# Softmax attention: the outputs of a head are turned by plain transposes in two halves, and VectorE adds the high and low parts

## The chip, the core and the metric

The kernel runs on one core of one Trainium2 chip. The metric is the device time of one execution in microseconds (us). The engines are TensorE (PE in the profile, its weight loads PEld), VectorE (DVE), ScalarE (ACT), GpSimd (POOL) and SyncE (SP, which issues the DMAs).

## What is computed

Four sublayers run one after the other over 2 x 1024 tokens of width 512: a gated delta-rule attention, a feed-forward with 4-bit weights, a latent attention with rotary embedding and softmax, and a feed-forward with 2:4 sparsity. The change is in the third, in the softmax part:

```python
attn = jnp.einsum('bqhd,bkhd->bhqk', q, k) * scale      # 16 heads, 16 numbers each for q and k
attn = jax.nn.softmax(attn, axis=-1)
out = jnp.einsum('bhqk,bkhd->bqhd', attn, v)            # 32 numbers per head
out = out.reshape(b, s, d)
return out @ wo
```

## The kernel before

`softmax_heads` works through 32 heads (16 heads of 2 sequences), 8 steps to a head, one for each tile of 128 keys or queries (`T` = 8). Each engine has a body written out for four heads (`QUAD`), in which `t` is the step; `passes` runs it once by itself (`first`), six times in a loop, and once more by itself (`last`). The order of the work on each engine is the order in which these bodies are written, and semaphores tie the engines together. In every step

- TensorE computes a tile of raw scores of a later head, 12 tiles ahead (`query_scores`, L1623, into the single PSUM tile `q_scores`). VectorE takes the maximum over the 1024 keys from it (`maximum`, L1557, a reduction of 128x1024). The next `query_scores` waits for that reduction (`max_done`).
- TensorE computes the next tile of transposed scores with the maxima subtracted (`key_scores`, L1639), ScalarE takes the exponential (L1511) and rounds 768 of its 1024 columns to a high part `p_hi` (L1500), and GpSimd computes the remainder `p_lo` (L1459).
- TensorE multiplies a tile of three steps earlier with the values (`output`, L1656 to L1658). The stationary operand holds high values in columns 0 to 31, low values in columns 32 to 63, and ones in 64 and 65. So rows 0 to 31 of the sum are the output by the high values, rows 32 to 63 by the low ones, and row 64 is the denominator.

Once per head the following comes in between. In step 3 of the next head ScalarE and VectorE copy the finished sums, [66 rows x 1024 queries], from PSUM to `out_t` (L1494, L1570). In step 4 TensorE transposes the maxima of the next head (`turn_top`, L1631) into the one PSUM bank `turned`, and VectorE copies them out (`copy_top`, L1564). Ahead of the `query_scores` of step 5, `turn_out` (L1660) waits for that copy and for both copies to `out_t`, and brings the head's sums to query-major form by eight fp32 matmuls (L1667): the stationary operand is a 128x128 block of `out_t`, the moving one is `fold`, [128 x 33], which holds two 32x32 identities above one another and a one for the denominator, so that the matmul turns the block and adds high and low part at once:

```python
for t in range(T):
    last = pe.matmul(turned[:, t * OUT_COLS:(t + 1) * OUT_COLS], out_t[:, t * P:(t + 1) * P], fold[:],
                     start=True, stop=True)
```

In step 6, after that step's reduction, `normalise_head` on VectorE takes the reciprocal of the eight denominators (L1577) and multiplies 128x256 numbers with them into `mixed` (L1580). `fold` is filled in the stage's beginning (L1531, L1545, L1546), and SyncE, TensorE, ScalarE and GpSimd wait for that beginning (`ones_done`).

## Time and profile before

| | us |
|---|---|
| median of 3 runs (3488.66 to 3490.54) | 3490.04 |
| the profiled execution | 3493.09 |
| its span in the trace | 3491.3 |
| attention stage of the change, from its first memset to the last multiplication | about 2177 to 2846.5 |
| of it, TensorE from first to last matmul | 2206.5 to about 2845.8 |

A time in the trace counts from the start of the span. Busy time is given per engine, with its share of the span; the idle time in front of an instruction is given in square brackets with the instruction that ended it. A matmul's recorded duration contains the way through the array, so that successive matmuls overlap in the record and TensorE can look busy where it waited; the start times of its weight loads (PEld) tell its pace.

### The profile page before, as it was taken

The page shows a single profiled execution, that of the slowest core. Times are in us where ns is not written, and L with a number is a line of the kernel's source. Part 1 is how long each engine was busy: PE and PEld are TensorE (multiplying, and loading weights), DVE is VectorE, ACT ScalarE, POOL GpSimd, SP SyncE. Part 2 cuts the span into 40 slices and gives each one's busy share as a digit, 9 for nine tenths or more (in the row PEclk, how much of TensorE's full clock was granted, in tenths as well). Part 3 has the DMA queues.
Part 4 walks back from the last instruction along what each step waited for, and adds up shares of the span by engine and source line. Part 5 has one row for each costly group of instructions (what it writes and reads, how often), then busy time and mean ns, then how long its engine had stood idle before and what let it go on. Part 6 is the DMA issues. An engine that isn't in the chain of part 4 may idle for free. (4 is left out here: it accounts for less than half of the span.)

```text
span 3491.3 us, 44228 instructions
## 1 busy us (share of the span) xinstructions
PE 3107.1 (89%) x16144; PEld 2588.9 (74%) x16144; DVE 1854.5 (53%) x2398; ACT 1176.3 (34%) x1731; POOL 809.2 (23%) x438
## 2 busy tenths in 40 slices
PE   5778888888869999999999965599999986999998
PEld 4667777777758888888888854388888865888887
DVE  5755555555464454454454454466655635554554
ACT  2323333333221121121111112277777752222221
POOL 0023333333200000000000002287888850000000
PEclk8978889999889999999999987699999998999999
DMA  2310000000010010010010002000000001000001
GB/s 93 111 37 20 21 20 21 20 21 7 7 50 23 18 32 22 18 34 20 18 35 19 1 5 114 31 29 27 30 27 28 25 13 48 13 37 24 12 12 48
DMA packets 45623, 104.09 MB, mean 30 GB/s; under 512 B 3600, under 2 KB 24080, under 8 KB 42704
## 3 DMA queue, kind: packets, MB, share of 16 engines
q1 hardware_dynamic: 45520, 102.62, 8.8%
q8 instruction: 76, 1.25, 0.1%
q14 instruction: 27, 0.22, 0.0%
HBM read 80.33 MB, written 22.02 MB: 29 GB/s over the span
## 5 line engine op out<-in xcount | busy, mean ns | idle before, releaser
L1459 POOL TENSOR_TENSOR att_p_lo<-att_probs,att_p_hi 128x768 fp32r<-128x768 f32 x256 | 467.2, 1836 | 159.4 <-ACT att_p_hi L1500 156.3
L1557 DVE TENSOR_REDUCE att_top<-att_q_scores 128x1 f32<-128x1024 f32 x250 | 305.8, 1223 | 240.3 <-PE att_q_scores L1623 233.0
L297 DVE TENSOR_TENSOR fp_hidden<-fp_gelu,fp_up 128x512 f32<-128x512 f32 x128 | 88.0, 687 | 447.9 <-PE fp_up L75 384.0
L1511 ACT ACTIVATE att_probs<-att_k_scores 128x1024 f32<-128x1024 f32 x256 | 262.6, 1026 | 169.4 <-PE att_k_scores L1639 165.2
L116 POOL MEMSET n1a_power<- 128x16 f32 x1 | 0.1, 111 | 1078.0 <-POOLq L52 1078.0
L1623 PE MATMUL att_q_scores<-att_k_stack,att_q_stack 128*128 128x512 f32 x500 | 191.6, 465 | 48.7 <-DMA att_q_stack<-att_k_stack 47.2
L286 DVE TENSOR_TENSOR k_stream<-k_stream,fp_down 128x512 f32<-128x512 f32 x256 | 175.5, 685 | 91.1 <-PE fp_down L75 87.5
L347 ACT ACTIVATE fp_gelu<-fp_gate 128x512 f32<-128x512 f32 x128 | 76.2, 596 | 422.0 <-PE fp_gate L75 421.1
L73 PE MATMUL fp_gate<-f_feat_hi,fp_w_hi 128*128 128x512 f32 x512 | 200.0, 391 | 13.8 <-DVE fp_w_lo L266 13.8
L1500 ACT CAST att_p_hi<-att_probs 128x768 fp32r<-128x768 f32 x256 | 211.5, 827 | 0.0
L808 POOL TENSOR_TENSOR dr_a_l<-dr_a_t,l_mask 128x1536 f32<-128x1536 f32 x48 | 172.1, 3593 | 143.7 <-PE dr_bank L1088 79.1
L74 PE MATMUL fp_gate<-f_feat_lo,fp_w_hi 128*128 128x512 f32 x512 | 199.9, 390 | 0.0
L75 PE MATMUL fp_gate<-f_feat_hi,fp_w_lo 128*128 128x512 f32 x512 | 199.8, 390 | 0.0
L75 PE MATMUL fp_up<-f_feat_hi,fp_w_lo 128*128 128x512 f32 x512 | 199.2, 389 | 0.0
L74 PE MATMUL fp_up<-f_feat_lo,fp_w_hi 128*128 128x512 f32 x512 | 199.2, 389 | 0.0
L73 PE MATMUL fp_down<-fp_w_hi,fp_h_hi 128*128 128x512 f32 x512 | 199.2, 389 | 0.0
L74 PE MATMUL fp_down<-fp_w_lo,fp_h_hi 128*128 128x512 f32 x512 | 199.2, 389 | 0.0
L75 PE MATMUL fp_down<-fp_w_hi,fp_h_lo 128*128 128x512 f32 x512 | 199.2, 389 | 0.0
L73 PE MATMUL fp_up<-f_feat_hi,fp_w_hi 128*128 128x512 f32 x512 | 199.2, 389 | 0.0
L1639 PE MATMUL att_k_scores<-att_q_stack,att_k_stack 128*128 128x512 f32 x512 | 166.7, 407 | 14.5 <-DMA att_q_stack<-att_top_rows 14.0
L957 DVE TENSOR_TENSOR dr_t_m<-dr_t_m,dr_bank 128x512 f32<-128x512 f32 x120 | 82.5, 688 | 180.0 <-PE dr_bank L1097 180.0
L1918 DVE TENSOR_TENSOR sp_hidden<-sp_silu,sp_up 128x512 f32<-128x512 f32 x64 | 43.9, 687 | 222.8 <-PE sp_up L75 221.7
(339 smaller groups left out, 7342.1 us busy)
## 6 DMA issues: line engine op xcount, KB each, us to landing
f_words<-codes SPq DMA_DIRECT2D x16, 768.0 KB
f_scale<-scales SPq DMA_DIRECT2D x16, 768.0 KB
f_staged<-w_sparse SPq DMA_DIRECT2D x12, 1024.0 KB, 4.8
qkv<-pc_rows SPq DMA_DIRECT2D x9, 1024.0 KB, 4.4
dr_raw<-qkv SPq DMA_DIRECT2D x16, 576.0 KB, 6.1
att_q_stack<-rotated SPq DMA_DIRECT2D x64, 128.0 KB
att_k_stack<-rotated SPq DMA_DIRECT2D x64, 128.0 KB
k_stream<-hidden SPq DMA_DIRECT2D x4, 1024.0 KB, 8.9
```

Of the source, the lines that this page charges most:

```text
L73: pe.matmul(out, w_hi, x_hi, start=start, stop=False)
L74: pe.matmul(out, w_hi, x_lo, start=False, stop=False)
L75: return pe.matmul(out, w_lo, x_hi, start=False, stop=stop)
L286: dve.tensor_tensor(tile, tile, down_ps[j][:], ALU.add).then_inc(added, 1)
L297: dve.tensor_tensor(hidden[:, c, :], gelu[:, c, :], up_ps[c][:], ALU.mult).then_inc(product_done, 1)
L808: pool.tensor_tensor(a_l[:, level % 2], a_t[:], const(LEVEL0 + level, BH), ALU.mult).then_inc(a_l_done, 1)
L1459: pool.tensor_tensor(p_lo[:, buffer, :], probs[:, slot, 0:SPLIT], p_hi[:, buffer, :].bitcast(F32), ALU.subtract).then_inc(lo_done, 1)
L1500: act.copy(p_hi[:, buffer, :], probs[:, slot, 0:SPLIT]).then_inc(hi_done, 1)
L1511: act.activation(probs[:, t, :], k_scores[:], ACT.Exp).then_inc(exp_done, 1)
L1557: dve.tensor_reduce(top[buffer][:, STACK + t:STACK + t + 1], scores[:], AX.XY, ALU.max, negate=True).then_inc(max_done, 1)
L1623: last = pe.matmul(scores[:, half, :], q_stack[j][:, t * P:(t + 1) * P], k_stack[j][:, half * TB:(half + 1) * TB], start=True, stop=True)
L1639: last = pe.matmul(k_scores[:, half, :], k_stack[j][:, t * P:(t + 1) * P], q_stack[j][:, half * TB:(half + 1) * TB], start=True, stop=True)
```

## The change

The eight matmuls with `fold` are replaced by eight plain transposes against the identity, each 128x128. Four of them fill the bank `turned` (4 x 128 columns), so that it goes in two halves: half 0 ahead of the `query_scores` of step 5, as before; half 1 ahead of the `query_scores` of step 7, after a wait until VectorE has finished with half 0. Since a transpose doesn't add the parts, VectorE does it. For each half it takes the reciprocal of four denominators, copies the low part from PSUM to SBUF, adds it to the high part within PSUM, and multiplies. Half 0 is done in step 6, half 1 in step 0 of the following head, each after that step's reduction. ScalarE's and VectorE's copies to `out_t` wait for one half each, and `fold` goes away.

```diff
-        fold = s.sb("fold", [P, OUT_COLS])
-        inverse = s.sb("inverse", [P, QTILES])
+        inverse = s.sb("inverse", [P, QTILES // 2])
+        low_part = s.sb("low_part", [P, QTILES // 2, HEAD_DIM1])
...
-            by_query = turned[:, 0:T * OUT_COLS].rearrange("p (t d) -> p t d", d=OUT_COLS)
-
-            def normalise_head(g, n, j):
-                dve.wait_ge(out_turned, g + 1)
-                dve.reciprocal(inverse[:], by_query[:, :, HEAD_DIM1]).then_inc(inverse_done, 1)
-                dve.wait_ge(inverse_done, g + 1)
-                dst = mixed[:, bass.ds(n, 1), :, HEAD_DIM1 * j:HEAD_DIM1 * (j + 1)].rearrange("p o t d -> p (o t) d")
-                dve.tensor_tensor(dst, by_query[:, :, 0:HEAD_DIM1],
-                                  inverse[:].unsqueeze(2).broadcast_to([P, T, HEAD_DIM1]), ALU.mult).then_inc(mixed_done, 1)
+            by_query = turned[:].rearrange("p (t d) -> p t d", t=T // 2)
+            upper, lower = by_query[:, :, 0:HEAD_DIM1], by_query[:, :, HEAD_DIM1:2 * HEAD_DIM1]
+
+            def normalise_half(g, n, j, half):
+                dve.wait_ge(out_turned, 2 * g + half + 1)
+                dve.reciprocal(inverse[:], by_query[:, :, 2 * HEAD_DIM1]).then_inc(inverse_done, 1)
+                dve.tensor_copy(low_part[:], lower).then_inc(lowered, 1)
+                dve.wait_ge(lowered, 2 * g + half + 1)
+                dve.tensor_tensor(upper, upper, low_part[:], ALU.add).then_inc(folded, 1)
+                dve.wait_ge(inverse_done, 2 * g + half + 1)
+                dve.wait_ge(folded, 2 * g + half + 1)
+                tiles = slice(half * T // 2, (half + 1) * T // 2)
+                dst = mixed[:, bass.ds(n, 1), tiles, HEAD_DIM1 * j:HEAD_DIM1 * (j + 1)].rearrange("p o t d -> p (o t) d")
+                dve.tensor_tensor(dst, upper, inverse[:].unsqueeze(2).broadcast_to([P, T // 2, HEAD_DIM1]),
+                                  ALU.mult).then_inc(mixed_done, 1)
...
+                        if t == 0 and not (first and j < 2):
+                            normalise_half(g - 2, n + (j - 2) // QUAD, (j - 2) % QUAD, 1)
                         if t == T - 2 and not early:
-                            normalise_head(g - 1, n - (j == 0), (j - 1) % QUAD)
+                            normalise_half(g - 1, n - (j == 0), (j - 1) % QUAD, 0)
...
             passes(dve, body)
+            normalise_half(HEADS - 2, PASSES - 1, QUAD - 2, 1)
             copy_out(HEADS - 1, False)
-            normalise_head(HEADS - 1, PASSES - 1, QUAD - 1)
+            for half in range(2):
+                normalise_half(HEADS - 1, PASSES - 1, QUAD - 1, half)
...
-            def turn_out(g, first):
-                if not first:
-                    pe.wait_ge(mixed_done, g)
-                pe.wait_ge(copied_act, g + 1)
-                pe.wait_ge(copied_dve, g + 1)
-                for t in range(T):
-                    last = pe.matmul(turned[:, t * OUT_COLS:(t + 1) * OUT_COLS], out_t[:, t * P:(t + 1) * P], fold[:],
-                                     start=True, stop=True)
+            def turn_out(g, half, first):
+                if half or not first:
+                    pe.wait_ge(mixed_done, 2 * g + half)
+                pe.wait_ge((copied_act, copied_dve)[half], g + 1)
+                for t in range(T // 2):
+                    at = half * TB + t * P
+                    last = pe.transpose(turned[:, t * P:(t + 1) * P], out_t[:, at:at + P], ident[:])
                 last.then_inc(out_turned, 1)
...
                         if t == 5 and not early:
                             if not (last and j == QUAD - 1):
                                 pe.wait_ge(top_copied, g + 2)
-                            turn_out(g - 1, first and j == 1)
+                            turn_out(g - 1, 0, first and j == 1)
+                        if t == T - 1 and not early:
+                            turn_out(g - 1, 1, False)
```

How this moves instructions is shown at two places. First TensorE before, from the end of step 4 to the `query_scores` of step 6 (`k_ident` is the identity, L1623 `query_scores`, L1639 `key_scores`, L1656 to L1658 `output`):

```order
L1658 MATMUL att_out_rest<-att_probs,att_whole_values 128x256
L1667 MATMUL att_turned<-att_fold,att_out_t 128x33 x8
L1623 MATMUL att_q_scores<-att_k_stack,att_q_stack 128x512 x2
L1639 MATMUL att_k_scores<-att_q_stack,att_k_stack 128x512 x2
L1656 MATMUL att_out_first<-att_p_hi,att_split_values 128x512
L1657 MATMUL att_out_rest<-att_p_hi,att_split_values 128x256
L1656 MATMUL att_out_first<-att_p_lo,att_split_values 128x512
L1657 MATMUL att_out_rest<-att_p_lo,att_split_values 128x256
L1658 MATMUL att_out_rest<-att_probs,att_whole_values 128x256
L1623 MATMUL att_q_scores<-att_k_stack,att_q_stack 128x512 x2
```

TensorE as changed, from the `query_scores` of step 6 to that of step 7 (in the changed file L1628 is `query_scores`, L1644 `key_scores`, L1661 to L1663 `output`; an equal group of four stands ahead of step 5):

```order
L1628 MATMUL att_q_scores<-att_k_stack,att_q_stack 128x512 x2
L1644 MATMUL att_k_scores<-att_q_stack,att_k_stack 128x512 x2
L1661 MATMUL att_out_first<-att_p_hi,att_split_values 128x512
L1662 MATMUL att_out_rest<-att_p_hi,att_split_values 128x256
L1661 MATMUL att_out_first<-att_p_lo,att_split_values 128x512
L1662 MATMUL att_out_rest<-att_p_lo,att_split_values 128x256
L1663 MATMUL att_out_rest<-att_probs,att_whole_values 128x256
L1672 MATMUL att_turned<-k_ident,att_out_t 128x128 x4
L1628 MATMUL att_q_scores<-att_k_stack,att_q_stack 128x512 x2
```

One group of eight ahead of step 5 has become a group of four ahead of step 5 and another ahead of step 7, in front of which nothing of the kind stood.

VectorE before, from the reduction of step 5 to the copy of step 3 of the next head:

```order
L1557 TENSOR_REDUCE att_top<-att_q_scores 128x1
L1551 COPY att_whole_values<-la_values 128x8x32
L1557 TENSOR_REDUCE att_top<-att_q_scores 128x1
L1577 RECIPROCAL att_inverse<-att_turned 128x8
L1580 TENSOR_TENSOR la_mixed<-att_turned,att_inverse 128x8x32
L1557 TENSOR_REDUCE att_top<-att_q_scores 128x1 x4
L1570 COPY att_out_t<-att_out_rest 128x512
```

VectorE as changed, from the reduction of step 6 to the same copy (L1552 is the reduction):

```order
L1552 TENSOR_REDUCE att_top<-att_q_scores 128x1
L1573 RECIPROCAL att_inverse<-att_turned 128x4
L1574 COPY att_low_part<-att_turned 128x128
L1576 TENSOR_TENSOR att_turned<-att_turned,att_low_part 128x4x32
L1581 TENSOR_TENSOR la_mixed<-att_turned,att_inverse 128x4x32
L1552 TENSOR_REDUCE att_top<-att_q_scores 128x1 x2
L1573 RECIPROCAL att_inverse<-att_turned 128x4
L1574 COPY att_low_part<-att_turned 128x128
L1576 TENSOR_TENSOR att_turned<-att_turned,att_low_part 128x4x32
L1581 TENSOR_TENSOR la_mixed<-att_turned,att_inverse 128x4x32
L1552 TENSOR_REDUCE att_top<-att_q_scores 128x1 x2
L1565 COPY att_out_t<-att_out_rest 128x512
```

Two operations between the reductions of steps 6 and 7 have become four there and four more between those of steps 0 and 1.

## Rows read from the trace of the kernel before

**Rows 1.** The page of the whole span: engines in total, clock in 40 slices.
```profile
span 3491.3 us, 44228 instructions
...
PE 3107.1 (89%) x16144; PEld 2588.9 (74%) x16144; DVE 1854.5 (53%) x2398; ACT 1176.3 (34%) x1731; POOL 809.2 (23%) x438
...
PEclk8978889999889999999999987699999998999999
```

**Rows 2.** Windows of the attention stage: busy time of each engine, clock.
```profile
core 0: us, PE busy (x) PEld busy (x) DVE busy (x) ACT busy (x) POOL busy (x), PEclk, DMA share, GB/s
2300.00:2500.00 200.00, 199.06 (x1029) 160.60 (x1027) 120.22 (x138) 155.49 (x191) 159.98 (x95) 1.00 0.08 28
```

**Rows 3.** Timeline of one ordinary step: start, duration, engine, line, operation, idle before.
```profile
2504.14 0.32 PEld L1623 LDWEIGHTS att_q_scores<-att_k_stack,att_q_stack 128*128 128x128 f32 x2
2504.14 0.75 PE L1623 MATMUL att_q_scores<-att_k_stack,att_q_stack 128*128 128x512 f32 x2
...
2504.92 1.22 DVE L1557 TENSOR_REDUCE att_top<-att_q_scores 128x1 f32<-128x1024 f32 x1 [0.84 <-PE att_q_scores L1623]
...
2505.19 0.40 PE L1656 MATMUL att_out_first<-att_p_hi,att_split_values 128*128 128x512 f32 x1
...
2506.20 0.32 PEld L1623 LDWEIGHTS att_q_scores<-att_k_stack,att_q_stack 128*128 128x128 f32 x2
```

**Rows 4.** Timeline, steps 4 and 5 of the same head: the turn as it is.
```profile
2511.42 1.22 DVE L1557 TENSOR_REDUCE att_top<-att_q_scores 128x1 f32<-128x1024 f32 x1 [1.00 <-PE att_q_scores L1623]
...
2512.67 0.29 DVE L1564 CAST att_top_rows<-att_turned 8x128 fp32r<-8x128 f32 x1
...
2513.01 1.86 PEld L1667 LDWEIGHTS att_turned<-att_fold,att_out_t 128*128 128x128 f32 x16 [0.33 <-DVE att_top_rows L1564]
...
2514.79 0.30 PEld L1623 LDWEIGHTS att_q_scores<-att_k_stack,att_q_stack 128*128 128x128 f32 x2
```

**Rows 5.** Timeline, steps 6 and 7 of the same head: the normalisation as it is.
```profile
2517.62 1.22 DVE L1557 TENSOR_REDUCE att_top<-att_q_scores 128x1 f32<-128x1024 f32 x1 [0.62 <-PE att_q_scores L1623]
...
2518.76 0.20 DVE L1577 RECIPROCAL att_inverse<-att_turned 128x8 f32<-128x8 f32 x1
2518.89 0.31 PEld L1623 LDWEIGHTS att_q_scores<-att_k_stack,att_q_stack 128*128 128x128 f32 x2
...
2519.08 0.42 DVE L1580 TENSOR_TENSOR la_mixed<-att_turned,att_inverse 128x256 f32 x1
...
2519.68 1.23 DVE L1557 TENSOR_REDUCE att_top<-att_q_scores 128x1 f32<-128x1024 f32 x1 [0.17 <-PE att_q_scores L1623]
```

**Rows 6.** Groups of VectorE, 2300 to 2800 us: busy, mean ns, idle before.
```profile
L1570 DVE COPY att_out_t<-att_out_rest 128x512 f32<-128x512 f32 x27 | 18.7, 691 | 10.8 <-PE att_out_rest L1658 10.8
...
L1564 DVE CAST att_top_rows<-att_turned 8x128 fp32r<-8x128 f32 x27 | 7.8, 289 | 0.8
```

**Rows 7.** Timeline of TensorE in the recurrence: twelve transposes, then matmuls.
```profile
639.85 1.60 PE L1105 MATMUL dr_bank<-k_ident,dr_t_m 128*128 128x128 f32 x12
641.29 2.84 PE L1088 MATMUL dr_bank<-dr_t_m,dr_a_l 128*128 128x128 f32 x24
```

**Rows 8.** Windows of a normalisation, TensorE only transposing (columns as in rows 2).
```profile
976.00:980.00 4.00, 3.23 (x17) 3.04 (x17) 3.14 (x7) 2.25 (x4) 0.00 (x0) 0.67 0.00 0
...
988.00:992.00 4.00, 2.45 (x16) 2.07 (x16) 4.00 (x8) 1.93 (x5) 0.00 (x0) 1.00 0.00 0
```

**Rows 9.** Timeline of the stage's beginning and end.
```profile
2192.90 0.37 DVE L1545 COPY att_fold<-k_ident 32x32 f32<-32x32 f32 x2
...
2831.93 1.97 PEld L1667 LDWEIGHTS att_turned<-att_fold,att_out_t 128*128 128x128 f32 x16
2833.81 0.30 PEld L1639 LDWEIGHTS att_k_scores<-att_q_stack,att_k_stack 128*128 128x128 f32 x2
...
2843.82 1.86 PEld L1667 LDWEIGHTS att_turned<-att_fold,att_out_t 128*128 128x128 f32 x16 [1.25 <-issue]
...
2845.83 0.21 DVE L1577 RECIPROCAL att_inverse<-att_turned 128x8 f32<-128x8 f32 x1 [2.13 <-PE att_turned L1667]
```

More of the change, by code:

```diff
@@ L1364 @@
 OUT_ROWS = 2 * HEAD_DIM1 + 2
-OUT_COLS = HEAD_DIM1 + 1
 AHEAD = QTILES + 4
@@ L1403, in softmax_heads @@
         out_done, copied_act, copied_dve = (s.sem(x) for x in ("out_done", "copied_act", "copied_dve"))
-        out_turned, inverse_done, mixed_done = (s.sem(x) for x in ("out_turned", "inverse_done", "mixed_done"))
+        out_turned, inverse_done, lowered, folded, mixed_done = (
+            s.sem(x) for x in ("out_turned", "inverse_done", "lowered", "folded", "mixed_done"))
         block = s.block()
@@ L1413, in softmax_heads @@
         REST = TB // 2
-        ONES_MADE = 11 + 3 * QUAD
+        ONES_MADE = 7 + 3 * QUAD
         def values_of(n, j):
@@ L1492, in copy_out @@
                 if not first:
-                    act.wait_ge(out_turned, g)
+                    act.wait_ge(out_turned, 2 * g - 1)
                 act.copy(out_t[:, 0:TB], out_first[:]).then_inc(copied_act, 1)
@@ L1530, in _ @@
                 dve.memset(top[b][:], 0.0).then_inc(ones_done, 1)
-            dve.memset(fold[:], 0.0).then_inc(ones_done, 1)
             dve.memset(split_values[:].bitcast(F32), 0.0).then_inc(ones_done, 1)
@@ L1536, in _ @@
                 dve.memset(k_stack[j][P // 2:, :].bitcast(F32), 0.0).then_inc(ones_done, 1)
-            dve.wait_ge(ones_done, 6 + 2 * QUAD)
+            dve.wait_ge(ones_done, 5 + 2 * QUAD)
             for j in range(QUAD):
@@ L1542, in _ @@
                 dve.tensor_copy(sums, ones[:, 0:4 * T].rearrange("p (t x) -> p t x", x=2)).then_inc(ones_done, 1)
-            for half in range(2):
-                rows = slice(half * HEAD_DIM1, (half + 1) * HEAD_DIM1)
-                dve.tensor_copy(fold[rows, 0:HEAD_DIM1], ident[rows, rows]).then_inc(ones_done, 1)
-            dve.tensor_copy(fold[TOP_ROW, HEAD_DIM1:OUT_COLS], ones[TOP_ROW, 0:1]).then_inc(ones_done, 1)
             def whole(g, n, j, first):
@@ L1568, in copy_out @@
                 if not first:
[L1569 removed]
+                    dve.wait_ge(out_turned, 2 * g)
                 dve.tensor_copy(out_t[:, TB:].rearrange("p (a q) -> p a q", a=2), out_rest[:, :, 0:REST])\
                    .then_inc(copied_dve, 1)
[L1573 to L1581 removed]
+            by_query = turned[:].rearrange("p (t d) -> p t d", t=T // 2)
[12 more added lines that the diff above has]
+                                  ALU.mult).then_inc(mixed_done, 1)
             def body(n, first, last):
@@ L1629, in turn_top @@
                 if not first:
-                    pe.wait_ge(mixed_done, g - 2)
+                    pe.wait_ge(mixed_done, 2 * g - 4)
                 pe.transpose(turned[0:STACK + T, 0:P], top[buffer][:], ident[:]).then_inc(top_turned, 1)
@@ L1699, in _ @@
                 output(HEADS - 1, 1, t, False)
-            turn_out(HEADS - 1, False)
+            for half in range(2):
+                turn_out(HEADS - 1, half, False)
 def project_out(nc, prefix, stream, ident, mixed, w_out, width):
```

1 line of the change is left out of this document (removed).

## The prediction

> **What bounds the kernel now.** I read the page first, for the size of things: TensorE is busy 89% of 3491.3 us, and its clock is mostly near full [rows 1]. The change touches one stage, so I then took the windows inside that stage. TensorE looks busy 199.06 of 200 us, VectorE 120.22, ScalarE 155.49, GpSimd 159.98, at a granted clock of 1.00 [rows 2], the 2.4 GHz level. That reads as a stage bound by TensorE's work. The timeline says otherwise. In an ordinary step the weight load for `query_scores` starts at 2504.14, the scores are there when VectorE's reduction starts at 2504.92, that one ends at 2506.14 (2504.92 + 1.22), and the next weight load starts at 2506.20 [rows 3]. So the step of 2.06 us is a round trip: 0.78 us from weight load to reduction, 1.22 us of reduction, 0.06 us back. There is one `q_scores` tile, so nothing overlaps this. VectorE idles 0.84 us of each step, and TensorE only seems full, because its recorded durations overlap. Whatever TensorE saves counts only where the round trip does not already hold it, and whatever VectorE adds is free only up to its gap of 0.84 us.
>
> Two places in a head leave the ordinary step:
> - Step 5, the turn. The copy of the maxima ends at 2512.96 (2512.67 + 0.29), the 16 weight loads of the eight fp32 matmuls (two passes each) run from 2513.01, and `query_scores` starts at 2514.79 [rows 4]. That is 1.78 us, with VectorE waiting: fully on the path.
> - Step 6, the normalisation. The reduction ends at 2518.84 (2517.62 + 1.22), the reciprocal is recorded from 2518.76 and the multiplication ends at 2519.50. `query_scores` of step 7 has left already at 2518.89, and the next reduction starts at 2519.68 [rows 5]. So it lies in VectorE's gap and costs nothing.
>
> **The change, part by part.** I call c the time from the start of the reciprocal to the end of the multiplication for one half.
>
> *Transposes.* Twelve 128x128 fp32 transposes take 1.44 us from start to start of what follows (641.29 - 639.85), 0.12 us each [rows 7]; a matmul with `fold` takes 1.78 / 8 = 0.22 us. Four transposes take 0.48 us. The Trainium skill (TensorE: Matmul & The Clock Gate, Terms) says that transpose mode is four times faster for fp32. By that, four would take 0.22 us and the sum would come out near 3489. The row shows a factor of 1.9 and decides.
>
> *Step 5.* The wait in front stays; four transposes stand where 16 passes stood: 0.48 - 1.78 = **-1.30 us** per head.
>
> *c.* The reciprocal takes 0.20 us as before [rows 5], its duration being nearly all fixed. The copy reads 128 PSUM numbers per row: L1564 does just that in 0.289 us, and L1570 with 512 numbers takes 0.691, so a number costs (0.691 - 0.289) / 384, about a nanosecond [rows 6]. The multiplication falls from 256 to 128 numbers: 0.42 - 0.13 = 0.29. The addition, which writes PSUM, has no row; I take 0.29 as for the others. An operation that waits for none starts 0.08 us before the one in front ends, as the reciprocal does behind the reduction; one that waits for its predecessor starts 0.12 us behind its end, as the multiplication does (2519.08 - 2518.96) [rows 5]. So c = 0.20 - 0.08 + 0.29 + 0.12 + 0.29 + 0.12 + 0.29 = 1.23 us. Bounds: 0.99 with no gap at the two waits; 1.36 if the addition in PSUM costs as much as 256 numbers, 0.42 [rows 5].
>
> *Step 7.* TensorE now waits for half 0, and behind it in its order stands `query_scores` of step 7, for which VectorE waits in turn. From the end of step 6's reduction: -0.08 to the reciprocal, c, 0.05 for the signal (2512.96 to 2513.01 [rows 4]), 0.48 for the transposes. Before, `query_scores` went 0.05 after the reduction. So it is late by c + 0.40 = **+1.63 us**.
>
> *Steps 0 and 1.* Half 1 is normalised behind step 0's reduction and lasts until c - 0.08 after it. The next reduction could start 0.84 us after it [rows 3]; now it starts at c - 0.16, 0.08 before the multiplication's end. It is late by c - 1.00 = **+0.23 us**, and with the round trip binding everywhere nothing is caught up.
>
> *Sum.* -1.30 + 1.63 + 0.23 = +0.56 us per head. There are 31 turns inside the steps; the last two run where no scores are left to compute, so that 29 cost this: 29 x 0.56 = +16.2. In those two TensorE does 1.88 us of passes (2831.93 to 2833.81 [rows 9]), now 0.96, with VectorE idle enough to hide c: -1.8. The stage's beginning loses the filling of `fold`, 0.37 us [rows 9] and two small operations, about -0.55 (estimate). Its end was 2.01 us from first weight load to reciprocal [rows 9] plus 0.74 to the end of the multiplication (2518.76 to 2519.50 [rows 5]); now two halves in series, each 2.01 - 1.78 + 0.48 + c = 1.94, and a signal: 3.93 less 2.75, +1.2. Together **+15.1 us**. GpSimd, ScalarE and SyncE get nothing to do: GpSimd works 160 of 200 us [rows 2], and steps that grow longer give it slack; the loads of q and k run heads ahead. The two copies to `out_t` stay in step 3, where all four waits are over.
>
> The profiled execution took 3493.09 us for a span of 3491.3, so it would show 3508.2; it lies 3.05 above the median of the runs, and the median would be 3490.04 + 15.1 = **3505.1 us**. With c open the sum is 58c - 56.2 us: 0 at c = 0.97, +1 at c = 0.99, +23 at c = 1.36.
>
> **The rivals.** About 0.2%, 7 us here, is what a measurement of this kernel can tell from no change.
> 1. *Gain and loss cancel.* c lies between 0.85 and 1.09, because the gaps at the waits vanish behind longer operations: +1 us at 0.99, so about 3491. For it: the two waits for VectorE's own results may be over sooner than the 0.12 seen behind an operation of 0.20 us. Against it: that gap holds register work that the changed loop keeps.
> 2. *TensorE's own work is the bound*, and so the kernel gets faster. Then the time removed counts in full and both chains on VectorE lie beside TensorE's work: 31 x (1.78 - 0.96) = -25.4, so 3465. It speaks for it that TensorE is busy 99.5% [rows 2]. It would decide if TensorE needed more than 2.06 us for its work of a step. Against it: each `query_scores` follows 0.05 to 0.06 us behind a reduction [rows 3, 5], also right behind the turn, where no backlog of VectorE's exists.
> 3. *Transposes four times faster.* Four in 0.22 us save another 0.26 at both places, 58 x 0.26 = 15.1, and a little at the end: 3489. Against it: 0.12 us each [rows 7].
> 4. *The clock falls.* TensorE will stand still for about 1.1 us in each head and transposes right behind. If that took the clock to its 1.2 GHz level for one step per head, the work of a step, at most 2.06 us, would double: up to 29 x 1.8 = 52, so 3557. Against it: a normalisation in which TensorE only transposes, busy 2.45 of 4 us, has the clock rise from 0.67 to 1.00 [rows 8]. The Trainium skill (TensorE: Matmul & The Clock Gate, Part 4: PE-mode transpose) says that transposes don't count as activity for the clock; by that this rival would gain weight, but the trace disagrees with its 0.67 to 1.00.
>
> **How the numbers follow.** Forecast (c above 1.09) 0.68; the first rival 0.15; the second 0.10; the third 0.03; the fourth 0.04. Slower by over 0.2%: 0.68 + 0.04 = 0.72. Within: 0.15 + 0.03 = 0.18. Faster: 0.10. The range takes in the forecast's upper bound (3490 + 23 and some for waits I have not seen) and the first and third rivals below: 3489 to 3516. It leaves out the second and the fourth, 0.14, and a little at the ends.
>
> **What would show it.** Right: `query_scores` of step 7 about 1.7 us behind the end of step 6's reduction instead of 0.05 [rows 5]; that of step 5 about 0.85 us behind step 4's reduction instead of 2.15 [rows 4]; the reduction of step 1 starting about 0.2 us late with no idle time in front; TensorE's weight loads for the transposes waiting for the multiplication; a head longer by 0.56 us; clock 1.00. Wrong: a multiplication that ends within 0.95 us of its reciprocal's start, reductions late in other steps, or a step shorter than 2.06 us anywhere.

## The result and the profile after

| | before | after |
|---|---|---|
| median of 12 runs | 3489.45 us | 3497.49 us |
| the profiled execution's span | 3491.3 us | 3493.5 us |
| attention stage, first memset to last multiplication | 670.4 us | 679.0 us |
| one head (mean of 28) | 18.92 us | 19.26 us |

The ratio is 1.0023 (95% interval 1.0014 to 1.0033): the change makes the kernel slower by 8.0 us, just over 0.2%. The median after is over twelve runs of which one took 8590.2 us, for a reason of which no trace was kept; the ratio leaves it out, and without it the median is 3496.90 us and the loss 7.5 us. The direction and the range of the prediction hold; its +15.1 us is about twice too much.

The stage went from 2176.06 to 2846.49 before and goes from 2171.02 to 2850.04 now, +8.6 us. Of this the 28 heads make 28 x 0.335 = 9.4. The two spans differ by only 2.2 us, because the same code outside the stage took 6.4 us less in this one execution; so I compare inside the stage. The windows of the stage (start:end, length, busy time of TensorE, its weight loads, VectorE, ScalarE, GpSimd; then clock, DMA share and GB/s), first 200 us as in [rows 2]:

```profile
2300.00:2500.00 200.00, 188.89 (x923) 146.26 (x922) 130.37 (x199) 152.51 (x186) 159.07 (x95) 1.00 0.07 27
```

TensorE now shows 11 us of idle time where it had 1, and the clock stays at 1.00. The view of the waits between 2300 and 2800 us (sum, times, longest) says for what it idles:

```profile
DVE att_top L1552 <- PE att_q_scores L1628: 145.6, 154, 1.4
...
PEld att_turned L1672 <- DVE la_mixed L1581: 31.3, 26, 1.2
...
DVE la_mixed L1581 <- DVE att_turned L1576: 10.1, 48, 0.2
PEld att_q_scores L1628 <- DVE att_top L1552: 7.4, 26, 0.3
```

L1672 are the transposes, L1581 is the multiplication, L1552 the reduction, L1628 `query_scores`. The second row is the new wait: 1.20 us in each head, between half 0 and half 1. The timeline shows it (start, duration, engine, line, operation, idle time before). First the turn, which answers to [rows 4]:

```profile
2511.30 1.22 DVE L1552 TENSOR_REDUCE att_top<-att_q_scores 128x1 f32<-128x1024 f32 x1 [0.99 <-PE att_q_scores L1628]
...
2512.89 0.42 PEld L1672 LDWEIGHTS att_turned<-k_ident,att_out_t 128*128 128x128 f32 x4 [0.32 <-DVE att_top_rows L1559]
...
2513.28 0.30 PEld L1628 LDWEIGHTS att_q_scores<-att_k_stack,att_q_stack 128*128 128x128 f32 x2
```

From 2512.89 to 2513.28 the four transposes hold `query_scores` up for 0.39 us, where the 16 passes of before held it for 1.78. Then steps 6 and 7, which answer to [rows 5], and steps 0 and 1:

```profile
2516.11 1.23 DVE L1552 TENSOR_REDUCE att_top<-att_q_scores 128x1 f32<-128x1024 f32 x1 [0.42 <-PE att_q_scores L1628]
2517.25 0.17 DVE L1573 RECIPROCAL att_inverse<-att_turned 128x4 f32<-128x4 f32 x1
2517.34 0.26 DVE L1574 COPY att_low_part<-att_turned 128x128 f32<-128x128 f32 x1
2517.64 0.30 DVE L1576 TENSOR_TENSOR att_turned<-att_turned,att_low_part 128x128 f32<-128x128 f32 x1
2518.13 0.29 DVE L1581 TENSOR_TENSOR la_mixed<-att_turned,att_inverse 128x128 f32 x1 [0.19 <-DVE att_turned L1576]
...
2518.47 0.42 PEld L1672 LDWEIGHTS att_turned<-k_ident,att_out_t 128*128 128x128 f32 x4 [1.20 <-DVE la_mixed L1581]
...
2518.86 0.30 PEld L1628 LDWEIGHTS att_q_scores<-att_k_stack,att_q_stack 128*128 128x128 f32 x2
...
2519.64 1.23 DVE L1552 TENSOR_REDUCE att_top<-att_q_scores 128x1 f32<-128x1024 f32 x1 [1.22 <-PE att_q_scores L1628]
...
2521.70 1.23 DVE L1552 TENSOR_REDUCE att_top<-att_q_scores 128x1 f32<-128x1024 f32 x1 [0.84 <-PE att_q_scores L1628]
...
2523.73 0.29 DVE L1581 TENSOR_TENSOR la_mixed<-att_turned,att_inverse 128x128 f32 x1 [0.21 <-DVE att_turned L1576]
2523.94 1.21 DVE L1552 TENSOR_REDUCE att_top<-att_q_scores 128x1 f32<-128x1024 f32 x1
```

The chain of a half takes 1.17 us (2517.25 to 2518.42), TensorE stands still for it, and VectorE in turn stands still for 1.22 us ahead of step 7's reduction. At step 1 the reduction follows the multiplication without a gap.

To have the whole head in numbers, I took the time from the start of one reduction to the start of the next, step by step, as the mean over 28 heads. This table is worked out from the start times in the timelines; the rows below the second are the experiments.

| kernel | 4-5 | 5-6 | 6-7 | 7-0 | 0-1 | 1-2 | 2-3 | 3-4 | head |
|---|---|---|---|---|---|---|---|---|---|
| before | 4.15 | 2.06 | 2.06 | 2.07 | 2.07 | 2.07 | 2.23 | 2.22 | 18.92 |
| after | 2.83 | 2.06 | 3.52 | 2.06 | 2.24 | 2.04 | 2.29 | 2.24 | 19.26 |
| late half | 2.83 | 2.06 | 2.22 | 2.34 | 2.24 | 2.04 | 2.28 | 2.23 | 18.23 |
| no addition | 2.83 | 2.06 | 2.94 | 2.06 | 2.06 | 2.07 | 2.29 | 2.22 | 18.52 |
| fold, in halves | 3.33 | 2.06 | 3.44 | 2.06 | 2.06 | 2.07 | 2.33 | 2.22 | 19.55 |
| chain split | 2.83 | 2.05 | 2.06 | 2.08 | 2.49 | 2.06 | 2.44 | 2.23 | 18.25 |
| in the gaps | 2.83 | 2.06 | 2.07 | 2.57 | 2.03 | 2.06 | 2.29 | 2.23 | 18.13 |
| copy back | 2.83 | 2.05 | 2.06 | 2.50 | 2.06 | 2.06 | 2.29 | 2.23 | 18.09 |
| short maximum | 3.94 | 2.05 | 2.06 | 2.06 | 2.06 | 2.06 | 2.23 | 2.22 | 18.67 |
| short both | 3.94 | 2.05 | 2.05 | 2.06 | 2.06 | 2.06 | 2.22 | 2.22 | 18.66 |

From before to after (differences of the unrounded means) the step 4-5 gives 1.33 us, 6-7 takes 1.46, 0-1 takes 0.17, of which 1-2 gives 0.03 back, and 2-3 and 3-4 take 0.07 together.

These means hide a difference between the passes. Of the 28 values of each interval, four lie in the first and the last pass, which are written out by themselves, and 24 in the loop (`passes`). In the written-out passes the change costs nothing: the seven intervals from step 4 to step 3 of the next head add up to 16.68 us before and after (I leave out 3-4, where one head of the change is 0.37 us longer for a reason that I haven't found). In the loop the head goes from 18.92 to 19.29 us, and 24 x 0.377 is 9.0 of the 9.4 us. The intervals of the change are 2.84 in the loop against 2.76 written out (4-5), 3.53 against 3.43 (6-7), 2.25 against 2.14 (0-1) and 2.30 against 2.20 (2-3). Half 0 of a head in the first pass:

```profile
2286.10 0.17 DVE L1573 RECIPROCAL att_inverse<-att_turned 128x4 f32<-128x4 f32 x1
2286.19 0.26 DVE L1574 COPY att_low_part<-att_turned 128x128 f32<-128x128 f32 x1
2286.48 0.30 DVE L1576 TENSOR_TENSOR att_turned<-att_turned,att_low_part 128x128 f32<-128x128 f32 x1
2286.89 0.29 DVE L1581 TENSOR_TENSOR la_mixed<-att_turned,att_inverse 128x128 f32<-128x128 f32 x1
2287.23 0.42 PEld L1672 LDWEIGHTS att_turned<-k_ident,att_out_t 128*128 128x128 f32 x4 [1.12 <-DVE la_mixed L1581]
```

The chain takes 1.08 us here (2286.10 to 2287.18) and 1.16 to 1.22 in the loop. The operations are as long; what differs is the gap in front of the multiplication, 0.10 us here and 0.19 to 0.25 there. The trace also records instructions on registers, which the views don't count. In all 48 chains of the loop one of VectorE's queue stands in that gap (at L1581), and in none of the other 16. It takes 0.040 to 0.094 us, and the gap is that duration and another 0.151 to 0.155 us in every case. In the source the waits of the loop compare with values worked out from the loop variable `n`, those of the written-out passes with constants. No run replaces these waits, so that their price in the total is read from the trace and not tested by itself.

### The profile page after: what moved, and what is told of

It is laid out like the page before. It is cut to its first block and busy times, and to the rows that moved or that the text cites. A ratio compares the mean times of both kernels' runs of the same rounds, so it can differ in the third digit from the quotient of the medians.

```text
span 3493.5 us, 44079 instructions
## 1 busy us (share of the span) xinstructions
PE 3087.2 (88%) x15888; PEld 2555.3 (73%) x15888; DVE 1889.7 (54%) x2586; ACT 1176.2 (34%) x1731; POOL 810.3 (23%) x438
## 5 line engine op out<-in xcount | busy, mean ns | idle before, releaser
L1459 POOL TENSOR_TENSOR att_p_lo<-att_probs,att_p_hi 128x768 fp32r<-128x768 f32 x256 | 469.4, 1841 | 166.2 <-ACT att_p_hi L1500 166.0
L1552 DVE TENSOR_REDUCE att_top<-att_q_scores 128x1 f32<-128x1024 f32 x250 | 305.4, 1222 | 205.2 <-PE att_q_scores L1628 197.3
L1628 PE MATMUL att_q_scores<-att_k_stack,att_q_stack 128*128 128x512 f32 x500 | 190.1, 462 | 48.3 <-DMA att_q_stack<-att_k_stack 46.8
L1644 PE MATMUL att_k_scores<-att_q_stack,att_k_stack 128*128 128x512 f32 x512 | 166.8, 407 | 14.8 <-DMA att_q_stack<-att_top_rows 14.5
```

The source lines that it names most:

```text
L1459: pool.tensor_tensor(p_lo[:, buffer, :], probs[:, slot, 0:SPLIT], p_hi[:, buffer, :].bitcast(F32), ALU.subtract).then_inc(lo_done, 1)
L1552: dve.tensor_reduce(top[buffer][:, STACK + t:STACK + t + 1], scores[:], AX.XY, ALU.max, negate=True).then_inc(max_done, 1)
L1628: last = pe.matmul(scores[:, half, :], q_stack[j][:, t * P:(t + 1) * P], k_stack[j][:, half * TB:(half + 1) * TB], start=True, stop=True)
L1644: last = pe.matmul(k_scores[:, half, :], k_stack[j][:, t * P:(t + 1) * P], q_stack[j][:, half * TB:(half + 1) * TB], start=True, stop=True)
```

## The experiments

The expectations speak of three theories. A: a step is a round trip between the engines, and what stands ahead of a reduction or of `query_scores` is paid in full. B: VectorE's added work costs wherever it stands. C: TensorE's own work is the bound. Each time is compared with runs of the kernel before on the same chip.

### Half 1 turned later

Only the place of half 1's turn moves, from step 7 to step 0 of the following head, one step further behind half 0's normalisation.

```diff
-                        if t == T - 1 and not early:
-                            turn_out(g - 1, 1, False)
+                        if t == 0 and not (first and j < 2):
+                            turn_out(g - 2, 1, False)
```

> The change, but half 1 is turned ahead of query_scores of step 0 of the next head instead of step 7; half 0 is still normalised behind step 6's reduction. Theory A (the step is a round trip between TensorE and VectorE, and the change pays for the wait ahead of step 7): TensorE finds half 0 done, so no wait of 1.2 us is left; per head -1.39 (step 5) + 0.39 (four transposes ahead of step 0) + 2 x 0.18 (each chain of 1.17 us overfills VectorE's gap) = -0.64, so about 3470. Theory B (what costs is VectorE's added work, wherever the wait stands): near the changed kernel, 3494 to 3500. Theory C (TensorE's own work is the bound): TensorE's work is that of the change, so also near 3497.

Measured: 3466.24 us, ratio 0.9934 (0.9917 to 0.9951), against 1.0023 for the change. Moving one call of four transposes by one step is worth about 31 us, and turns the loss into a gain. VectorE does the same work as in the change, so B falls. The interval 6-7 goes from 3.52 to 2.22. What remains above 2.06 there is the multiplication, which again ends just before the reduction:

```profile
2527.62 0.29 DVE L1581 TENSOR_TENSOR la_mixed<-att_turned,att_inverse 128x128 f32 x1 [0.19 <-DVE att_turned L1576]
2527.83 1.21 DVE L1552 TENSOR_REDUCE att_top<-att_q_scores 128x1 f32<-128x1024 f32 x1
```

### Without the addition

The kernel leaves out the low part: the copy to `low_part` and the addition, with their two waits, are gone.

```diff
-                dve.tensor_copy(low_part[:], lower).then_inc(lowered, 1)
-                dve.wait_ge(lowered, 2 * g + half + 1)
-                dve.tensor_tensor(upper, upper, low_part[:], ALU.add).then_inc(folded, 1)
                 dve.wait_ge(inverse_done, 2 * g + half + 1)
-                dve.wait_ge(folded, 2 * g + half + 1)
```

> The change without the copy of the low part and without the addition (so the output lacks the low part of the values' product). The chain of a half falls from 1.17 to about 0.6 us. Theory A: the wait ahead of step 7 shortens one for one, by 0.57, and step 1 is no longer late (0.17): -0.74 x 29 = -21, so about 3476. Theory C: VectorE's work lies beside TensorE's, no change: 3497.

Measured: 3472.2 us, 0.9953 (0.9936 to 0.9969). With the chain shorter by 0.57 us (1.17 to 0.60), 6-7 shrinks by just that (3.52 to 2.94), and the delay of 0-1 is gone (2.06), since 0.6 us fits into VectorE's gap of 0.84. So the length of the chain is paid one for one at step 7, and at step 0 only what exceeds the gap.

### The old fold matmuls, in two halves

This keeps the split but lets the matmuls with `fold` add the parts, as before, so that VectorE has only reciprocal and multiplication.

```diff
-                    last = pe.transpose(turned[:, t * P:(t + 1) * P], out_t[:, at:at + P], ident[:])
+                    last = pe.matmul(turned[:, t * OUT_COLS:(t + 1) * OUT_COLS], out_t[:, at:at + P], fold[:],
+                                     start=True, stop=True)
```

> The change's two halves and their places, but each half is turned by four matmuls with fold, as before, so that nothing is copied or added. Theory A: step 5 saves 0.89, step 7 costs the chain of 0.6 + 0.31 + 0.50 for the longer turn = 1.41, steps 0 and 1 nothing: +0.52 per head, x 29 = +15, about 3504: slower than either kernel, though nothing was added to VectorE but one reciprocal and one operation's fixed part. Theory B: as the kernel before, 3489 to 3493.

Measured: 3506.4 us, 1.0051 (1.0034 to 1.0068). So it is the split into halves that costs, with the wait for half 0 in it; the plain transposes themselves gain. Four `fold` matmuls against four transposes: 3.33 to 2.83 in 4-5, that is 0.50 us.

### The chain split in two

Half 1 is turned at step 1, and each chain is cut behind the copy: reciprocal and copy (`take_half`) at steps 6 and 1, addition and multiplication (`finish_half`) at steps 7 and 2.

```diff
-                        if t == 0 and not (first and j < 2):
-                            normalise_half(g - 2, n + (j - 2) // QUAD, (j - 2) % QUAD, 1)
-                        if t == T - 2 and not early:
-                            normalise_half(g - 1, n - (j == 0), (j - 1) % QUAD, 0)
+                        if t == 1 and not (first and j < 2):
+                            take_half(g - 2, 1)
+                        if t == 2 and not (first and j < 2):
+                            finish_half(g - 2, n + (j - 2) // QUAD, (j - 2) % QUAD, 1)
+                        if t == T - 2 and not early:
+                            take_half(g - 1, 0)
+                        if t == T - 1 and not early:
+                            finish_half(g - 1, n - (j == 0), (j - 1) % QUAD, 0)
```

> The change with the work put where the gaps are: half 1 is turned ahead of query_scores of step 1 of the next head, and VectorE's chain is cut in two, reciprocal and copy behind one reduction (0.35 us), addition and multiplication behind the next (0.7 us), so that each piece fits VectorE's gap of 0.84 us. It leaves nothing out. Theory A: step 5 stays 1.32 shorter than before, four transposes cost 0.39 ahead of step 1, and no reduction is late: -0.9 per head, x 29 = -26 and about -2 in the last heads, so about 3461, 5 us below the version with the late half. Theory B (VectorE's added work costs wherever it stands): near that version, 3466.

Measured: 3468.8 us, 0.9941 (0.9925 to 0.9958), some 8 us more than I expected. The two intervals of half 0 are free (2.06, 2.08). But the transposes cost 0.42 at 0-1, and in step 3 the finishing of half 1 runs into VectorE's copy to `out_t`, L1565, so that 2-3 is longer by another 0.15:

```profile
2532.26 0.29 DVE L1587 TENSOR_TENSOR la_mixed<-att_turned,att_inverse 128x128 f32 x1 [0.25 <-DVE att_turned L1582]
2532.47 0.69 DVE L1565 COPY att_out_t<-att_out_rest 128x512 f32<-128x512 f32 x1
2533.08 1.21 DVE L1552 TENSOR_REDUCE att_top<-att_q_scores 128x1 f32<-128x1024 f32 x1
```

### Both chains in gaps of their own

Half 0 is taken at step 5 and finished at step 6; half 1 is turned and taken at step 0 and finished at step 1. To make room at step 5, the copy of the values (L1546) moves to step 7.

```diff
+                        if t == 0 and not (first and j < 2):
+                            take_half(g - 2, 1)
+                        if t == 1 and not (first and j < 2):
+                            finish_half(g - 2, n + (j - 2) // QUAD, (j - 2) % QUAD, 1)
+                        if t == T - 3 and not early:
+                            take_half(g - 1, 0)
+                        if t == T - 2 and not early:
+                            finish_half(g - 1, n - (j == 0), (j - 1) % QUAD, 0)
...
-                        if t == BEHIND + 2 and not (last and j == QUAD - 1):
+                        if t == T - 1 and not (last and j == QUAD - 1):
                             whole(g + 1, n + (j + 1) // QUAD, (j + 1) % QUAD, early)
```

> The version cut in two, with its pieces moved to steps whose gap is free: half 0 is taken (reciprocal, copy) behind step 5's reduction and finished behind step 6's, the copy of the next head's values moves from step 5 to step 7, half 1 is turned ahead of query_scores of step 0 of the next head, taken behind step 0's reduction and finished behind step 1's, two steps before the copy to out_t of step 3. It leaves nothing out. If the 0.2 us that the version before it lost between steps 2 and 3 come from the finish of half 1 and the copy to out_t meeting in one gap, the head takes 18.92 - 1.32 + 0.39 = 18.0 us, and the kernel about 3461. If VectorE's added work costs wherever it stands, 3466 to 3469, as the two versions before.

Measured: 3465.12 us, 0.9923 (0.9910 to 0.9937). Every step is short but 7-0, with 2.57. There the copy of the values takes 1.53 us where it took 0.28 before (the next kernel shows that this is not why the interval is long). Beside it runs the first of two GpSimd instructions L1459 (1.84 us each), from 2525.45:

```profile
2524.75 0.75 POOL L1464 TENSOR_TENSOR att_split_values<-la_values,att_split_values 128x256 fp32r<-128x256 f32 x1
2524.78 1.23 DVE L1552 TENSOR_REDUCE att_top<-att_q_scores 128x1 f32<-128x1024 f32 x1
2525.45 3.68 POOL L1459 TENSOR_TENSOR att_p_lo<-att_probs,att_p_hi 128x768 fp32r<-128x768 f32 x2
2525.92 1.53 DVE L1546 COPY att_whole_values<-la_values 128x256 f32 x1
2527.36 1.21 DVE L1552 TENSOR_REDUCE att_top<-att_q_scores 128x1 f32<-128x1024 f32 x1
```

I took this copy for the cause of the 2.57, and put it back to step 5 in the next kernel, with no other edit.

> The kernel of the run before in which both halves' chains stand in gaps (half 0 taken at step 5 and finished at step 6, half 1 turned ahead of query_scores of step 0, taken there and finished at step 1), with one edit: the copy of the values (line 1546) goes back from step 7 to step 5, where the changed kernel has it and where it took .41 us. If theory A (round trip plus what stands ahead of a reduction) holds and the copy beside GpSimd's instruction was what made the interval 7-0 2.57 us long, that interval falls to 2.34 to 2.45 (the chain of half 1's transposes, 4 x .10, ahead of the weight load, as in the run with the late half), 5-6 stays within 2.06 to 2.15, the head is 18.0 us, and the time is near 3461 us (3458 to 3463). If the copy takes 1.5 us at step 5 too, the time is 3465 or more. Theory C (TensorE's own work sets the steps) allows no gain over the run before.

Measured: 3465.93 us, 0.9924 (0.9911 to 0.9938); the two kernels can't be told apart. The copy takes 0.41 us again, but 7-0 is still 2.50, so my reading was wrong: the copy accounts for 0.07 at most. VectorE has nothing to do in the 1.27 us ahead of this reduction. It is TensorE that comes late:

```profile
2523.82 0.31 PEld L1638 LDWEIGHTS att_q_scores<-att_k_stack,att_q_stack 128*128 128x128 f32 x2
...
2525.57 0.59 PE L1673 MATMUL att_out_rest<-att_probs,att_whole_values 128*128 128x256 f32 x2
2525.78 0.58 PEld L1682 LDWEIGHTS att_turned<-k_ident,att_out_t 128*128 128x128 f32 x4
...
2526.33 0.30 PEld L1638 LDWEIGHTS att_q_scores<-att_k_stack,att_q_stack 128*128 128x128 f32 x2
...
2527.10 1.23 DVE L1552 TENSOR_REDUCE att_top<-att_q_scores 128x1 f32<-128x1024 f32 x1 [1.27 <-PE att_q_scores L1638]
```

From one `query_scores` to the next it is 2.51 us, and in this stretch the trace names no wait in front of any TensorE instruction: an ordinary step of 2.06 and 0.45 for four transposes. If a step were only a round trip with slack on TensorE, some of the 0.45 would be absorbed. None is. Here theory A, as I had used it, is not enough.

### Shorter maximum, shorter exponential

To see what TensorE needs by itself, the reduction of the kernel before takes only the first 512 of 1024 keys, and the exponential is scaled by 0.001 to stay finite.

```diff
-                dve.tensor_reduce(top[buffer][:, STACK + t:STACK + t + 1], scores[:], AX.XY, ALU.max,
+                dve.tensor_reduce(top[buffer][:, STACK + t:STACK + t + 1], scores[:, 0:1, :], AX.XY, ALU.max,
```

> The kernel before, with a maximum over 512 of the 1024 keys and the exponent scaled by 0.001 so that it stays finite (the maxima of the other half are left out, the softmax is another one). The reduction falls from 1.22 to 0.69 us and the round trip from 2.06 to 1.53. Theory A: the step shortens until the next bound, TensorE's own work of some 1.8 to 2.0 us or the loop through the exponential: -0.05 to -0.25 us in each of some 240 steps, 12 to 60 us faster (3430 to 3478). Theory C (TensorE's own work is the bound): within 5 us of before.

Measured: 3482.57 us, 0.9976 (0.9966 to 0.9986). The reduction takes 0.69 us instead of 1.22, and the ordinary step stays 2.06. Only 4-5 shrinks, by 0.21, since the copy of the maxima comes earlier. Theory A asked for a gain of at least 12 us and shorter steps, and fell. Theory C had the steps right, but allowed 5 us and so missed the turn's part. One other loop was left as a suspect, ScalarE's with `k_scores`, so the next kernel also takes the exponential over 512 of 1024 queries; the rest of `probs` is left at 1.

> The kernel before with the short maximum, and with the exponential of 512 instead of 1024 numbers (the other half of the probabilities is a constant 1, set once). With the short maximum alone the ordinary step stayed at 2.06 us. If what held it there is the loop from key_scores through the exponential (0.97 + 1.02 + 0.06 us), the step now falls to TensorE's own work, between 1.8 and 2.0 us, and the time by 0.06 to 0.26 us in some 220 steps, to 3425 to 3470. If what held it is TensorE's own work, the step stays within 0.02 us of 2.06 and the time within 5 us of 3482.

Measured: 3485.73 us, 0.9986 (0.9976 to 0.9995), with steps of 2.05 to 2.06 again (the time is above the last one's because this stage begins with an additional memset of 6.0 us, for `probs`). A step of it:

```profile
2497.29 0.41 PEld L1624 LDWEIGHTS att_q_scores<-att_k_stack,att_q_stack 128*128 128x128 f32 x2
...
2498.17 0.69 DVE L1558 TENSOR_REDUCE att_top<-att_q_scores 128x1 f32<-128x512 f32 x1 [1.18 <-PE att_q_scores L1624]
...
2498.64 0.60 ACT L1511 ACTIVATE att_probs<-att_k_scores 128x512 f32<-128x512 f32 x1 [0.75 <-PE att_k_scores L1640]
...
2499.36 0.41 PEld L1624 LDWEIGHTS att_q_scores<-att_k_stack,att_q_stack 128*128 128x128 f32 x2
```

The reduction ends at 2498.86, half a microsecond before `query_scores` starts again, and still the step is 2.07 us. In this stretch the trace names no wait in front of a TensorE instruction. So TensorE's own work for a step takes 2.06 us, the same as the round trip.

### Filling VectorE's gap

Four kernels add memsets to the kernel before, on a tile that nothing reads, behind the reduction of step 1: one of 512 columns, eight of 64, 24 of 21, 48 of 10.

```diff
+                        if t == 1:
+                            for q in range(48):
+                                dve.memset(idle[:, 10 * q:10 * (q + 1)], 0.0)
```

> The kernel before, with one memset of 128x512 unused numbers on VectorE behind step 1's reduction in each head, some 0.5 to 0.65 us, which is less than the gap of 0.84 us. Theory A: nothing, 3487 to 3492. Theory B (added work on VectorE costs by itself): 31 x 0.5 = +15, about 3505.

> The same unused 512 numbers in eight memsets of 64, with eight times the fixed part: in all some 1.0 to 1.7 us behind step 1's reduction. Theory A: the reduction of step 2 starts late by what goes over the gap, that length less 0.76 us, and it is never caught up: 30 times that, +6 to +28 us (3495 to 3517), and the lengthening of the interval between the reductions of steps 1 and 2 accounts for all of it. Theory C: no change.

> The kernel before with 24 memsets of 21 unused numbers behind step 1's reduction. Eight of 64 took 0.63 us and cost nothing; 24 should take between 1.2 and 1.9 us, over the gap of 0.84 us by 0.4 to 1.1. If the reduction is on the path, the interval between the reductions of steps 1 and 2 grows by just that excess, in 30 heads, and nothing is caught up: 3501 to 3523. If TensorE's own work is the bound and the reduction only keeps pace with it, the next steps catch up: under 3493.

> The kernel before, with 48 memsets of 128x10 (to a tile that nothing reads) on VectorE behind the reduction of step 1. By the run of 24 memsets, which took .75 us, they should take 1.5 us: .65 us more than the .84 us for which VectorE is idle there. Theory A: the step is a round trip as well, so the excess lengthens the interval 1-2 from 2.07 to 2.7 us, and the head by as much if nothing catches up behind it: 29 x .65 = +19, near 3508 us. If later steps catch up (there is slack in the buffers between TensorE and VectorE), the interval 2-3 or 3-4 shortens below 2.2 and the time stays under 3500 us. If TensorE's own work alone sets the step and VectorE has slack, nothing changes: 3490 us.

Measured: 3490.40, 3490.16, 3489.82 and 3490.75 us; ratios 1.0002 (0.9993 to 1.0012), 1.0000 (0.9990 to 1.0010), 0.9999 (0.9990 to 1.0008) and 1.0000 (0.9990 to 1.0009). The last three were meant to exceed the gap, and none did: small memsets take far less than I had scaled, 48 of them 0.90 us together.

```profile
2506.01 0.90 DVE L1596 MEMSET att_idle<- 128x10 f32 x48
...
2506.90 1.22 DVE L1558 TENSOR_REDUCE att_top<-att_q_scores 128x1 f32<-128x1024 f32 x1
```

At 48 the gap is just full: the reduction follows without idle time, the interval 1-2 is longer by 0.013 us and 2-3 shorter by 0.011. So the series shows that work up to the edge of the gap is free, and does not test what a larger excess costs. For that the only evidence is the 0.17 to 0.18 us at 0-1 in the change and in the kernel with the late half, and its absence without the addition.

## Why the prediction was right in direction and twice too large

**"What bounds the kernel now".** I wrote that the step is a round trip and that "TensorE only seems full". The first half stands, the second fell. With both of the other loops shortened a step stays 2.06 us, so round trip and TensorE's own work are nearly equally long (2.065 us a step before, 2.056 with both shortened). My argument had been that `query_scores` starts 0.06 us behind each reduction [rows 3]; that shows that the round trip binds, by about 0.01 us, not that TensorE has slack. The sum did not suffer, because the change makes TensorE idle.

**Rival 1** (gain and loss cancel, c between 0.85 and 1.09) is what happened in the written-out passes: c is 1.08 there, and the seven intervals add up to the same before and after. In the loop c is 1.16 to 1.22 and the forecast holds. What the prediction set against this rival, that the gap holds register work which the changed loop keeps, is borne out at the second wait (0.19 to 0.25 us) and not at the first (0.034 to 0.036 us in all 64 chains).

**Rival 2** had the right premise and the wrong consequence. It took both chains as hidden beside TensorE's work and came to 3465 us. They are not hidden in the change, since TensorE must wait for one of them. Where they are placed so that they are, the kernels take 3465.12 and 3465.93 us, which is what that rival says. It gives the simplest account of the change: with no chain exposed the head falls from 18.92 to 18.09 us (copy back), a gain of 0.83; against that kernel the change has 1.02 more at step 7 (6-7 and 7-0 together), where TensorE waits for the chain, and 0.15 more at steps 0 to 2, 1.17 in all; net +0.34 us.

**Step 5**, predicted -1.30, measured -1.33 in the mean. Two errors offset: four transposes take 0.39 us (2512.89 to 2513.28), not 0.48, which would give -1.39; in 12 of 28 heads the interval is about 2.92 instead of 2.76, and there the profile names "issue" ahead of L1672, up to 0.5 us, and no other engine. The trace records an instruction on registers of TensorE's queue there, at L1668, 0.17 us ahead of the first weight load. These 12 heads are all of the loop.

**c**, predicted 1.23 (0.99 to 1.36), measured 1.17 in the head shown; in the mean of the loop 1.18 for half 0 and 1.20 for half 1, and 1.08 outside it. By operation: reciprocal 0.17 for 0.20, copy 0.26 for 0.29, addition in PSUM 0.30 for 0.29, multiplication 0.29 for 0.29, and the gaps 0.04 and 0.19 for twice 0.12 (that their sum agrees is luck: one was too long and the other too short). The groups of VectorE between 2300 and 2800 us (busy and mean ns behind the bar) show the mean durations:

```profile
L1576 DVE TENSOR_TENSOR att_turned<-att_turned,att_low_part 128x128 f32<-128x128 f32 x52 | 15.6, 299 | 1.8
L1581 DVE TENSOR_TENSOR la_mixed<-att_turned,att_inverse 128x128 f32 (+1 forms) x52 | 15.2, 292 | 10.5 <-DVE att_turned L1576 10.1
L1574 DVE COPY att_low_part<-att_turned 128x128 f32<-128x128 f32 x52 | 13.5, 259 | 0.0
L1546 DVE COPY att_whole_values<-la_values 128x256 f32 (+1 forms) x26 | 10.5, 405 | 0.0
L1573 DVE RECIPROCAL att_inverse<-att_turned 128x4 f32<-128x4 f32 x52 | 8.9, 171 | 0.0
```

**Step 7**, "c + 0.40 = +1.63", measured +1.46. The mechanism is the predicted one. By its own terms with the measured sizes: 1.17 - 0.08 + 0.05 + 0.39 - 0.05 = 1.48. `query_scores` starts 1.52 us behind the end of step 6's reduction (2517.34 to 2518.86); I had said about 1.7.

**Steps 0 and 1**, "c - 1.00 = +0.23", measured +0.17 in the mean of all 28: +0.19 in the loop, near 1.20 - 1.00, and +0.07 outside it, near 1.08 - 1.00. Of that 0.03 is caught up in 1-2; "nothing is caught up" holds nearly.

**Not foreseen:** +0.05 at 2-3 and +0.02 at 3-4. The first appears in every kernel with the turn in two halves, without the addition too, and in none of the others. The trace shows where it arises: the two copies to `out_t` start about 0.41 us behind the weight load of step 3's `query_scores` in the loop, where before they start 0.33 behind it in three of four heads and 0.42 in the fourth. Each late pair has an instruction on registers right in front (L1493, L1564), and the pairs on time have none; outside the loop no pair is late. The waits at these lines compare with `2 * g - 1` and `2 * g`, where they compared with `g` before. By the prediction's own list, late reductions in other steps and a step shorter than 2.06 us (2.04 at 1-2) were signs of its being wrong; both appeared, each at no more than 0.05 us.

**The sum.** +0.335 per head against +0.56: of the difference of 0.225, step 7 makes 0.17, steps 0 to 2 0.09 and step 5 0.03, less 0.07 at 2-3 and 3-4 (the rest is rounding). Over 28 heads that is 6.3 us, close to the 7.1 us by which the prediction was off. The late copies, which the sum put at nothing, made the miss smaller by 0.07. The term of the sum that was mis-sized most was that of step 7, by two small errors of the same sign, the transposes (0.09) and c (0.06); both are multiplied by the number of heads. Since the gain and the loss are each near 1.5 us and the net is their difference, a tenth of a microsecond in a term moves the result by 3 us.

**Rival 3** falls with 0.39 us for four transposes. The Trainium skill (TensorE: Matmul & The Clock Gate, Terms) gives transpose mode a factor of four for fp32; a `fold` matmul took 0.22 us and a transpose takes 0.10, a factor of 2.3. A `fold` matmul moves 33 columns only, but like against like gives no more: in the recurrence of the kernel before, twelve fp32 matmuls of 128x128 take 2.68 us (641.29 to 643.97), 0.22 each, and twelve transposes 1.44, a factor of 1.9.

**Rival 4** falls: TensorE idles 1.11 to 1.42 us and transposes right behind it in each head, at a granted clock of 1.00 from 2250 to 2850 us. What the prediction set against it was weaker than it looked. The windows of [rows 8] are means of two levels, and between the two shown the clock went down and up again while TensorE only transposed: 0.50 from 976 to 978 us, 1.00 from 979 to 982, 0.50 from 983 to 985 and 1.00 from 986 to 994.

## What to carry to other kernels

Splitting a hand-over through one buffer into two puts the consumer's whole chain between the halves, on the producer's queue, and what is queued behind that wait is late as well. Leave at least one full step between the consumer's start and the second half, and check each slot on the consumer for what already stands there: the same edit was +8 us with the halves two steps apart and -23 us with three. An engine that always starts right behind another one's signal may still be full; only shortening the other's work tells.

A wait in a loop can bring an instruction on registers with it, when the value that it waits for depends on the loop variable. Here one of 0.04 to 0.09 us stands in each chain. On a chain that another engine waits for it counts in full; compare a written-out pass with the loop to see it.

## What the runs showed of the hardware

A VectorE copy of 128x256 fp32 from SBUF to SBUF took 283 ns in the kernel before, 405 in the change, and 1500 in the mean in the kernel where it stood beside GpSimd's L1464 and L1459; the reduction and copies from PSUM showed nothing of the kind (the reduction over 1024 took 1.21 to 1.23 us in all kernels). In the kernel before no GpSimd instruction runs beside it between 2300 and 2800 us. The mean of 405 hides two groups, 0.32 to 0.34 and 0.48 to 0.51 us (one copy took 0.42), and what they have in common with the 1.5 us is the end: between 2300 and 2800 us in the change and in the kernel with both chains in gaps, each copy issued while GpSimd's L1459 ran (53 of 54) ended 0.146 to 0.154 us behind that instruction's end, however long before it had been issued. The Trainium skill (SBUF — State Buffer, Who interferes with whom) says that GpSimd and a VectorE copy in a two-port mode lock a shared pair of ports against each other for a whole instruction; by that rule a copy issued 0.47 us into a GpSimd instruction of 1.84 us waits for that instruction's end, and the trace agrees (2525.45 + 1.84 = 2527.29, and the copy ends at 2527.45).

Small VectorE memsets behind each other cost far less than single operations do: 48 of 128x10 took 0.90 us, 19 ns each, while an operation of 128x4 on PSUM took 171 ns.
